# Cross-attention with the value products of both groups of a batch done together in the second group, and key copies ahead of the transposes in the first

## The reference

```python
x = x + xattn(layernorm(x), ctx, Wq, Wk, Wv, Wo)    # x (32, 64, 512), ctx (32, 512, 384)
# inside xattn, 16 heads of 32 columns:
q = (x @ Wq); k = (context @ Wk); v = (context @ Wv)
scores = jnp.einsum('bhid,bhjd->bhij', q, k) * scale
attn = jax.nn.softmax(scores, axis=-1)
out = jnp.einsum('bhij,bhjd->bhid', attn, v)
return out.reshape(B, N, 512) @ Wo
```

## Time and profile before

| | before |
|---|---|
| time, median of 3 runs | 1203.17 us (1202.5 to 1204.98) |
| the profiled execution's own time | 1203.76 us |
| its span | 1202.0 us |
| PE busy | 1185.2 us, 99% |
| VectorE busy | 749.6 us, 62% |
| ScalarE busy | 623.8 us, 52% |
| GpSimd busy | 599.8 us, 50% |
| transfers `turned<-blocks` issued by SP, by ScalarE | 840, 120 |

### The profile page before, as it was taken

How to read it: one execution, slowest core, us unless ns; L and a number is a source line. 1 busy time by engine, 2 the same in 40 slices (tenths; PEclk the granted TensorE clock), 3 DMA queues, 4 the chain that set the end, 5 groups by cost and what they waited for, 6 DMA issues and landing times.

```text
span 1202.0 us, 32636 instructions
## 1 busy us (share of the span) xinstructions
PE 1185.2 (99%) x12300; PEld 944.3 (79%) x12300; DVE 749.6 (62%) x1833; ACT 623.8 (52%) x1232; POOL 599.8 (50%) x331
## 2 busy tenths in 40 slices
PE   7999999999999999999999999999999999999998
PEld 6877777777777777777777777898888887888886
DVE  4256657656756756666666665558877888527223
ACT  6456556656656656656566566752222336434431
POOL 6922342432532533523524429467666664665663
PEclk9999999999999999999999999999999999999999
DMA  8045554555555555455455453200100013343431
GB/s 291 29 136 136 154 137 133 147 138 137 139 139 146 129 140 155 124 134 156 126 136 153 128 145 104 72 23 20 28 20 20 20 37 107 120 136 116 165 122 62
DMA packets 89314, 137.01 MB, mean 114 GB/s; under 512 B 20768, under 2 KB 25120, under 8 KB 89248
## 3 DMA queue, kind: packets, MB, share of 16 engines
q1 hardware_dynamic: 82208, 124.01, 36.6%
q10 hardware_dynamic: 5760, 7.87, 2.8%
q0 software_dynamic: 1280, 4.20, 1.0%
HBM read 63.39 MB, written 6.29 MB: 58 GB/s over the span
## 4 chain that ended last, share of the span: by engine, by line
PE 93%; DVE 3%; POOL 2%; issue 1%; ACT 1%; DMA 0%; POOLq 0%; SPq 0%; DVEq 0%
PE psum L220 44%; PE psum L1876 7%; PE psum L2216 7%; PE psum L1137 6%; PE psum L238 6%; PE psum L249 5%; PE psum L294 4%; PE psum L1165 3%; PE psum L875 3%; PE psum L1126 3%; PE psum L1178 1%; PE psum L1221 1%; POOL sm L1585 1%; PE psum L280 1%; PE psum L2190 1%
## 5 line engine op out<-in xcount | busy, mean ns | idle before, releaser
L418 DVE CUSTOM_DVE_ANT_0 prob<-psum,mbias 128x512 f32<-128x512 f32 x256 | 165.4, 684 | 202.8 <-PE psum L238 202.8
L336 ACT ACTIVATE prob<-prob,nmx 128x512 f32<-128x512 f32 x256 | 182.7, 714 | 102.1 <-DVE nmx L418 71.2
L342 ACT ACTIVATE prob<-prob,rinv 128x512 f32<-128x512 f32 x256 | 176.3, 712 | 0.0
L596 POOL TENSOR_SCALAR ctx_a<-ctx_r 128x1536 fp32r<-128x1536 f32 x16 | 65.5, 4092 | 216.4 <-DMA ctx_r<-in_ctx 196.4
L441 DVE STREAM_TRANSPOSE blocks<-prob 128x512 f32<-128x512 f32 x240 | 163.1, 699 | 12.5 <-ACT prob L342 12.5
L596 POOL TENSOR_SCALAR ctx_b<-ctx_r 128x1536 fp32r<-128x1536 f32 x16 | 65.4, 4088 | 186.9 <-PE psum L220 159.7
L367 ACT ACTIVATE V<-psum 128x512 f32<-128x512 f32 x120 | 71.7, 598 | 166.3 <-PE psum L220 166.3
L220 PE MATMUL psum<-ctx_b,wk_h 128*128 128x512 f32 x384 | 127.2, 398 | 0.0
L220 PE MATMUL psum<-ctx_a,wk_h 128*128 128x512 f32 x384 | 126.8, 398 | 0.0
L220 PE MATMUL psum<-wv_h,ctx_b 128*128 128x512 f32 x384 | 124.8, 391 | 0.2 <-DVE K L433 0.2
L220 PE MATMUL psum<-wv_h,ctx_a 128*128 128x512 f32 x384 | 124.1, 390 | 0.2 <-DVE K L433 0.2
(11 more groups left out here) (256 smaller groups left out, 2838.4 us busy)
## 6 DMA issues: line engine op xcount, KB each, us to landing
turned<-blocks SPq DMA_DIRECT2D x840, 64.0 KB
ctx_r<-in_ctx SPq DMA_DIRECT2D x32, 768.0 KB
w_r<-in_L_ffn_W SPq DMA_DIRECT2D x64, 256.0 KB, 2.8
turned<-blocks ACTq DMA_DIRECT2D x120, 64.0 KB
xres<-in_x SPq DMA_DIRECT2D x16, 256.0 KB, 2.6
out<-tok SPq DMA_DIRECT2D x16, 256.0 KB, 2.0
pX<-squares SPq DMA_DIRECT2D x52, 64.0 KB, 2.0
tok<-in_x SPq DMA_DIRECT2D x3, 1024.0 KB, 11.9
```

The costliest lines, as they stand in the source:

```text
L336: act.activation(prob[:, r, :], prob[:, r, :], ACT.Exp, bias=nmx[:, r:r + 1], scale=-1.0, accum_out=rsum[:, r:r + 1]).then_inc(s_ex, 1)
L342: act.activation(prob[:, r, :], prob[:, r, :], ACT.Copy, scale=rinv[:, r:r + 1]).then_inc(s_pn, 1)
L418: dve.tensor_tensor_reduce(prob[:, r, :], S_bank[r], mbias[:, b, :], 1.0, 3.0e38, ALU.add, ALU.min, nmx[:, r:r + 1]).then_inc(s_mx, 1)
L596: pool.tensor_scalar(y[:, 0], ctx_r[:], 1.0, None, ALU.mult).then_inc(s_cx, 1)
```

## The change

Value products: an even group has none. An odd group q has those of z = q - 3 and z = q - 2 one behind the other (`values_of_two`), in two halves of `PV_bank`, behind a wait for both exchanges. `s_PV` is still counted up once for each. One copy on ScalarE and one subtraction on VectorE, twice as wide, take both out. ScalarE's two transfers for an even group move into the next, odd group, between that copy and the first normalization (in tile 0, group 0 keeps its own place). VectorE's block transposes wait for the landed exchange of two groups before, and no longer for `s_PV`. In even groups, and in all groups of tile 0, VectorE's key copies stand ahead of block transposes 0 and 1. SP's code is the same. Tile 15 is the same.

```diff
--- before.py
+++ after.py
@@ -239,6 +239,17 @@
                                     KT_sb[rows, 2 * a + c, :], start=True, stop=True, tile_position=(r * HD, c * SQ))
             ins.then_inc(s_S, 1)
 
+        def values_of_two(pe, g, q, first=False):
+
+            i, z = GPT * g + q, (q - 3) % GPT
+            for e in range(2):
+                pe.wait_ge(s_ex4[z + e], 256 * (g + 1 if q >= 2 else g))
+            if not (first and q == 3):
+                pe.wait_ge(s_Ol, i - 3)
+            for e in range(2):
+                value_products(pe, z + e, lambda c, kt, r: turned[e][:, 2 * c:2 * c + 2, r, kt, :],
+                               PV_bank[:, e * 2 * SQ:(e + 1) * 2 * SQ])
+
         def value_products(pe, z, source, place):
 
             b, a = z // HALVES, z % HALVES
@@ -261,13 +272,12 @@
             pe.wait_ge(s_Ol, i - 1)
             value_products(pe, z, lambda c, kt, r: PT[:, r, kt, c * SQ:(c + 1) * SQ], place)
 
-        def pe_exchanged_values(pe, g, q, first=False):
+        def pe_exchanged_values(pe, g, q):
 
 
             i, z = GPT * g + q, (q - 2) % GPT
             pe.wait_ge(s_ex4[z], 256 * (g + 1 if q >= 2 else g))
-            if not (first and q == 2):
-                pe.wait_ge(s_Ol, i - 2)
+            pe.wait_ge(s_Ol, i - 2)
             value_products(pe, z, lambda c, kt, r: turned[z % 2][:, 2 * c:2 * c + 2, r, kt, :], PV_bank)
 
         def pe_turn(pe, g, q, r):
@@ -297,8 +307,8 @@
 
         def pe_group(pe, g, q, first=False):
             pe_scores(pe, g, q, first)
-            if not (first and q < 2):
-                pe_exchanged_values(pe, g, q, first)
+            if q % 2 and not (first and q == 1):
+                values_of_two(pe, g, q, first)
             pe_item(pe, g, q, 0)
             pe_item(pe, g, q, 1)
             if q == 1 and not first:
@@ -353,11 +363,32 @@
             b, a = z // HALVES, z % HALVES
             return x[:, 2 * a:2 * a + 2, b, :]
 
-        def act_outputs(act, g, q, lag, first=False, place=PV_bank):
+        def outputs_of_two(x, q):
+
+            return x[:, :, (q - 3) % GPT // HALVES, :]
+
+        def two_in_bank():
+
+            return PV_bank[:, 0:4 * SQ].rearrange("p (c n) -> p c n", c=4)
+
+        def act_outputs_of_two(act, g, q, first):
+
+            act.wait_ge(s_PV, GPT * g + q - 1)
+            if q == 3 and not first:
+                act.wait_ge(s_Wo, g)
+            act.activation(outputs_of_two(OT_h, q), two_in_bank(), ACT.Copy).then_inc(s_Oh, 2)
+
+        def dve_outputs_of_two(dve, g, q):
+
+            dve.wait_ge(s_Oh, GPT * g + q - 1)
+            dve.tensor_tensor(outputs_of_two(OT_l, q), two_in_bank(), outputs_of_two(OT_h, q).bitcast(F32),
+                              ALU.subtract).then_inc(s_Ol, 2)
+
+        def act_outputs(act, g, q, lag, place=PV_bank):
 
             z = (q - lag) % GPT
             act.wait_ge(s_PV, GPT * g + q - lag + 1)
-            if z == 0 and not first:
+            if z == 0:
                 act.wait_ge(s_Wo, g)
             act.activation(outputs_part(OT_h, z), place[:, 0:2 * SQ].rearrange("p (c n) -> p c n", c=2),
                            ACT.Copy).then_inc(s_Oh, 1)
@@ -369,8 +400,9 @@
         def act_group(act, g, q, first=False):
             act_exp(act, g, q, 0)
             act_exp(act, g, q, 1)
-            if not (first and q < 2):
-                act_outputs(act, g, q, 2, first)
+            if q % 2 and not (first and q == 1):
+                act_outputs_of_two(act, g, q, first)
+                act_exchange(act, g, q - 1, first)
             act_norm(act, g, q, 0)
             act_exp(act, g, q, 2)
             act_norm(act, g, q, 1)
@@ -379,7 +411,8 @@
             act_norm(act, g, q, 3)
             act_item(act, g, q, 2)
             act_item(act, g, q, 3)
-            act_exchange(act, g, q, first)
+            if q % 2 or (first and q == 0):
+                act_exchange(act, g, q, first)
 
         def act_last_group(act, g, q, fill=None, turn_sooner=False, between_turns=None):
             act_exp(act, g, q, 0)
@@ -437,7 +470,7 @@
             i = GPT * g + q
             dve.wait_ge(s_pn, 4 * i + r + 1)
             if r == 0 and not (first and q < 2):
-                dve.wait_ge(s_PV, i - 1)
+                dve.wait_ge(s_ex4[(q - 2) % GPT], 256 * (g + 1 if q >= 2 else g))
             dve.transpose(blocks[q % 2][:, :, r, :, :].rearrange("p g k n -> p k g n"),
                           prob[:, r, :].rearrange("p (k g n) -> p k g n", g=4, n=HD)).then_inc(s_bl, 1)
 
@@ -455,14 +488,22 @@
             dve_inverse(dve, g, q, 0)
             dve_max(dve, g, q, 3)
             dve_inverse(dve, g, q, 1)
-            if not (first and q < 2):
-                dve_outputs(dve, g, q, 2)
-            dve_blocks(dve, g, q, 0, first)
-            dve_item(dve, g, q, 0)
-            dve_inverse(dve, g, q, 2)
-            dve_blocks(dve, g, q, 1)
-            dve_inverse(dve, g, q, 3)
-            dve_item(dve, g, q, 1)
+            if q % 2 and not (first and q == 1):
+                dve_outputs_of_two(dve, g, q)
+            if first or q % 2 == 0:
+                dve_item(dve, g, q, 0)
+                dve_blocks(dve, g, q, 0, first)
+                dve_inverse(dve, g, q, 2)
+                dve_item(dve, g, q, 1)
+                dve_inverse(dve, g, q, 3)
+                dve_blocks(dve, g, q, 1)
+            else:
+                dve_blocks(dve, g, q, 0, first)
+                dve_item(dve, g, q, 0)
+                dve_inverse(dve, g, q, 2)
+                dve_blocks(dve, g, q, 1)
+                dve_inverse(dve, g, q, 3)
+                dve_item(dve, g, q, 1)
             dve_blocks(dve, g, q, 2)
             dve_blocks(dve, g, q, 3)
             if q == 1 and not first:
```

## The result

| | before | after |
|---|---|---|
| time, median | 1202.93 us (1202.50 to 1204.98, 4 runs) | 1213.95 us (1213.24 to 1214.55, 4 runs) |
| the profiled execution, its span | 1203.76, 1202.0 us | 1213.69, 1211.9 us |

The change makes the kernel slower: the ratio is 1.0083, with a 95% interval of 1.0071 to 1.0095. The prediction was 1218 us, with a range of 1206 to 1228.

What follows compares the result with a forecast made beforehand. TensorE was taken as the bound, with 93% of the chain that ended last. The terms -0.2 + 2.95 + 2.01 + 12.84 + 0.59 - 3.8 gave +14.4 us on 1203.76, so 1218 us was predicted, range 1206 to 1228.

Steps and rivals of the forecast that it cites:

- tile 0: Four groups of tile 0: 40.65 us, a wait of 1.13 included, against 40.82 before; -0.2 us.
- wait from tile 0 to 1, from 1 to 2: TensorE's waits before group 1's values in tiles 1 and 2, with SyncE's issues slower there: 2.95 and 2.01 us.
- twelve more waits: TensorE's wait before group 1's values in twelve further tiles, 1.07 us each: 12.84 us.
- last tile: The last tile still takes group 2's exchange in its group 0: 12.95 against 12.36 us, 0.59 us of wait.
- seam saving, 14 tiles: Doubled value products in odd groups save 0.135 us a pair of groups, 0.27 a tile, 3.8 us in all.
- The chain of the wait: From group 3's start through SyncE's two exchanges to group 1's values: 22.83 us; TensorE, ready at 21.76, waits 1.07.
- It repeats in every tile: The 1.07 us wait recurs in every tile, because the chain hangs on TensorE's own progress, not SyncE's.
- the first rival: Exchanges land in time and no wait is left: 1198.7 us; a chain 5% shorter is enough; chance 0.09.
- 28 issues from 78.54, end at 98.90: In tile 0, the exchanges of groups 0 and 1 end at 98.90, so group 3's values wait 1.13 us.
- The key copies: Odd groups: copy ends 7.1 to 7.2 us in, wanted at 7.24; even groups: keys first avoids losing 0.58 us each.
- The rule weighed: Skill's rule: starting a DMA is usually small, so postponing exchanges is free; set aside for 9.09 us per 14 issues.
- The slow rival: SyncE's issues get slower in the double exchange, 1.3 us more per tile, 18 us in all: 1236 us; chance 0.15.

Runs made afterwards that it cites:

- e1: The changed kernel, with a third buffer of its own for group 2's exchange: 1203.76 us against 1204.12 for the kernel before, ratio 0.9993.
- e2: The changed kernel, with the load of `xres` issued behind group 3's exchange instead of in front of it: 1204.68 us, ratio 1.0005 to the kernel before.
- e3_odd_all_sync: The changed kernel, with SyncE issuing all 16 transfers in odd groups and ScalarE none: 1245.64 us, ratio 1.0341 to the kernel before.
- e8_odd_one_more: The changed kernel, with SyncE issuing 15 transfers in odd groups and ScalarE one: 1222.89 us, ratio 1.0149 to the kernel before.
- e4: The changed kernel, with VectorE's key copies back behind the block transposes in all groups: 1226.66 us, ratio 1.0187 to the kernel before.
- experiment 5: The kernel before, with only the key copies put ahead of block transposes 0 and 1 in even groups and tile 0: 1203.56 us, ratio 0.9992.
- e6_own_buffer_act_back: The kernel of e1, with ScalarE's two transfers back at the end of every group: 1205.38 us, ratio 1.0011 to the kernel before.

## Why the prediction was right, point by point

The mechanism and the sign were right; most sizes were too large. The terms of the sum, as predicted and as read from the starts of the groups:

| term | predicted | measured |
|---|---|---|
| tile 0 | -0.2 | +0.8 |
| wait from tile 0 to 1, from 1 to 2 | 2.95 + 2.01 | 1.46 + 1.36 |
| twelve more waits | 12 x 1.07 = 12.84 | 12 x 0.70 = 8.4 |
| last tile | 0.59 | 0.2 |
| seam saving, 14 tiles | -3.8 | -2.9 |
| rest of the kernel | 0 | +0.6 |
| sum | +14.4 | +9.9 (the spans differ by 9.9) |

- **The chain of the wait.** Every link predicted is in the profile after, in the order given. All but one were a little shorter: 2.29 for 2.33, 8.87 for 9.09, 0.96 for 1.05, 8.75 for 8.83. The landing took 1.61 for 1.53, and PE was ready at 21.80 for 21.76. The chain is 22.48 us where 22.83 was said, an error of 1.5%, and for a wait that is the difference of two such numbers 1.07 us were predicted where 0.68 were measured. The prediction had noted that 1.07 of 22.83 us decides. The term that is off most is the first exchange's 9.09 us, for which 8.87 were measured; what makes an exchange of the same 14 issues take 8.75 in one place and 9.09 in another was not tried.
- **It repeats in every tile.** Right, 14 times, and the row of link lengths in experiments 1, 2, 3 and 8 shows it. e1 and e2 also show why the first rival (the exchanges land in time) was near: 0.68 us of order in SP's queue was enough for it.
- **Tiles 0 to 2.** The step "28 issues from 78.54, end at 98.90" failed. Those issues now take 18.43 us, from 78.19 to 96.62, not the 20.36 of the earlier trace rows, and the products of g3 follow their scores at once, so the wait of 1.13 us did not come. Why they were slow before and are not now was not tried by itself. In its place stood the stop of 1.67 us, which made g3 1.96 us longer than a group with a pair is, and which no row of before could have shown, since before there are no 128 products in a row. This same stop is also why the wait from tile 0 to 1 was half of its 2.95 us, and not a quicker chain. Of SP's next two exchanges the first was slower than the 10.29 us predicted:

```profile
100.27 11.71 SPq L591 DMA_DIRECT2D turned<-blocks  x14
...
112.81 8.75 SPq L591 DMA_DIRECT2D turned<-blocks  x14
```

  From the start of g3 at 98.01 the chain is 2.26 + 11.71 + 0.83 + 8.75 + 1.66 = 25.21 us. PE stopped inside it and needed 13.29 + 9.43 + 1.04 = 23.76, so 1.45 us were left to wait. Without the stop PE would have needed 21.80 and waited 3.4 us (an estimate from these rows). So the stop cost the kernel after next to nothing: tile 0 and the wait behind it give 0.8 + 1.46 = 2.2 us together, where 2.75 were predicted. In `e1_own_buffer`, where no wait follows that could hide it, the stop and the slower clock behind it make g3 of tile 0 4.1 us longer than a steady one. From tile 1 to 2 the two exchanges took 9.55 and 8.74 us, an excess of 0.7 over the steady ones where 0.94 was said.
- **The seam.** 128 products last 1.92 us in the chain, as predicted. The group without products is 9.43 us and not 9.40 (36 matmuls take 8.38 us behind scores and 8.36 behind values), and the saving is 0.21 us a tile, 44.45 - (44.94 - 0.70), not 0.27; without the waits, in e1, it is 0.22.
- **The key copies.** Both steps held. In odd groups no wait appeared: ScalarE slipped one of its issues into an exponential's time, and the key copy ended 6.6 us into its group, earlier than the 7.1 to 7.2 said. In even groups the cover works, and e4 prices it at 0.80 us a group, where 0.58 was said.
- **The rule weighed.** The prediction went by the row in which 14 issues hold SP for 9.09 us, and took it that such a queue cannot be put off for free. The Trainium skill (DMA: Bandwidth & Descriptors, section Issuing engines are not separate DMA queues) calls the time to start a DMA usually small beside the DMA. The runs disagree: an issue of 0.63 us stands beside the 1.98 us that the chain shows for the last transfer, 14 issues hold the queue for 8.87 us while the products start 1.61 us after the end of the last one, and an issue more adds its 0.63 us to the kernel's wait. The rival built on that rule did not come.
- **The slow rival** (issues get slower) did not come either: 28 issues take 17.98 us at 349.96, less than the 18.77 of the earlier trace rows.

## What to carry to other kernels

When work is moved to a later place, look first at what it frees: a buffer released one group later puts everything that fills it in series behind the new place, and the queue that issues those transfers may have no reserve although its engine shows no busy time. Add that chain up against the consumer's own pace, and treat a small difference between the two long sums as a sign with a wide size; then a reordered load or a small third buffer can be worth more than the change. A reordering that measures as nothing by itself (the key copies, experiment 5) can still be what a second change stands on (experiment 4).

## What the runs showed of the hardware that was not expected

- An idle stretch of PE can cost more than itself. After 1.85 to 1.90 us (`e3_odd_all_sync`, tiles 7 to 14) and 2.43 us (`e8_odd_one_more`, tile 2) the granted clock fell to 0.50 for some 3 us and the group lost 1.6 us more. After 0.7 and 1.3 us it stayed at 1.00. Stops of 1.94 us in an earlier tile, of 2.46 us in tile 0 of `e8_odd_one_more` and of 2.49 us in tile 0 of `e6_own_buffer_act_back` left it whole as well, so the length of the stop alone does not decide.
- PE can stop for 0.65 to 2.85 us with no semaphore behind it, after its first long run of short matmuls outside a loop, and single sets in that place make the stop go away. The cause is open.
- A transfer of 64 KB between partitions costs SP's queue 0.63 to 0.65 us on average in the steady loop (8.75 to 9.09 us for 14), up to 0.84 us in tile 0 (11.71 for 14), and it is this, not the bytes, that limits the exchange: experiments 3 and 8 move the same bytes.
